# A four-layer kernel on one core: first stage on bare ternary matrices, its first chunk projected early, and unused matrix products in two preparations

## The reference

```
xn = layernorm(x)
# attention part: gates, a linear recurrence over time, a gated MLP
h   = rms_norm(xn) ;  gate = gelu(h Wg + bg) ;  hs = h Wh + bh
r, i = sigmoid(h Wr + br), sigmoid(h Wi + bi)
a   = exp(-8 softplus(alpha) r) ;  s = sqrt(1 - a*a) * hs * i
o_t = a_t * o_(t-1) + s_t                      # scan over the tokens of a sequence
hs2 = o * gate + xn ;  h2 = rms_norm(hs2)
attn = (h2 Wfc + b) * gelu(h2 Wmg + b) @ Wout + bout + hs2
# feed-forward part, on xn: weights rounded to -1, 0, 1 and scaled by row
bitlinear(x, w): scale = max(mean|w|, 1e-5) ; x @ (clip(round(w/scale), -1, 1) * scale).T
h = bitlinear(xn, w_fc) + gate0 * (xn V' B' U')          # rank 16
ffn = bitlinear(relu(h)**2, w_proj)
x = x + attn + ffn
# second layer: a selective scan (mamba) and 8 experts, top 2 of 8
```

## Time and profile before

| | us |
|---|---|
| median of 3 runs | 2524.14 (2521.16 to 2524.48) |
| the profiled execution, whole | 2515.11 |
| its span, first to last instruction | 2513.2 |
| PE busy | 2127.5 (85%) |
| DVE busy | 1925.2 (77%) |
| ACT busy | 1364.5 (54%) |
| POOL busy | 1208.3 (48%) |

### The profile page before, as it was taken

The page is one execution under the profiler, slowest core; times in us unless marked ns, Lnnn a source line. Parts: engine busy times, 40 slices in busy tenths (PEclk is TensorE's granted clock), DMA queues, the critical chain, the costliest instruction groups (busy, mean ns, idle before and its releaser), DMA issues. The chain is left out here.

```text
span 2513.2 us, 38213 instructions
## 1 busy us (share of the span) xinstructions
PE 2127.5 (85%) x12306; PEld 1716.6 (68%) x12306; DVE 1925.2 (77%) x2430; ACT 1364.5 (54%) x2421; POOL 1208.3 (48%) x889
## 2 busy tenths in 40 slices
PE   2699999999977778787878888866599999999995
PEld 1577777787752445455545555545499999999995
DVE  6554565545642899999999999999498888888883
ACT  1332233222324576767676676654377777777772
POOL 1112221122201879889797979797123333333333
PEclk8899999999988879898989798967799999999998
DMA  8010111101122322232323232323266666666663
GB/s 269 17 43 0 42 42 42 42 0 42 42 69 71 106 76 80 102 109 72 121 78 104 78 122 79 100 93 132 91 217 232 230 206 232 226 209 233 225 207 88
DMA packets 108983, 286.86 MB, mean 114 GB/s; under 512 B 20550, under 2 KB 85462, under 8 KB 90022
## 3 DMA queue, kind: packets, MB, share of 16 engines
q1 hardware_dynamic: 94598, 267.12, 30.5%
q0 software_dynamic: 14304, 18.75, 3.6%
HBM read 239.21 MB, written 50.82 MB: 115 GB/s over the span
## 5 line engine op out<-in xcount | busy, mean ns | idle before, releaser
L1102 POOL TENSOR_TENSOR m_work<-m_ux,m_bb 128x1024 f32<-128x1024 f32 x256 | 600.1, 2360 | 72.4 <-DVE m_hh L1411 63.8
L1259 ACT ACTIVATE m_da<-m_dl,m_A 128x512 f32<-128x512 f32 (+1 forms) x512 | 332.1, 681 | 198.7 <-DVE m_hh L1411 197.4
L1852 PE MATMUL e_h<-e_xTh,e_w1h 128*128 128x256 f32 x1248 | 353.2, 283 | 8.2 <-DVE e_xTl L1788 6.7
L1852 PE MATMUL e_h<-e_xTl,e_w1h 128*128 128x256 f32 x1248 | 349.2, 280 | 0.0
L1852 PE MATMUL e_h<-e_xTh,e_w1l 128*128 128x256 f32 x1248 | 349.1, 280 | 0.0
L1421 DVE TENSOR_TENSOR m_work<-m_hh,m_cb 128x1024 f32<-128x1024 f32 x256 | 312.7, 1221 | 37.3 <-PE m_cb L1502 16.0
L1531 PEld LDWEIGHTS m_y<-m_ident,m_work 128*128 128x128 f32 x2048 | 289.9, 162 | 56.8 <-issue 40.2
L1531 PE MATMUL m_y<-m_ident,m_work 128*128 128x128 f32 x2048 | 323.9, 310 | 1.2 <-DVE m_work L1421 1.2
L1411 DVE TENSOR_TENSOR_SCAN m_hh<-m_da,m_carry,m_work 128x1024 f32<-128x1024 f32 x128 | 300.0, 2344 | 6.4 <-ACT m_work L1270 6.4
L1411 DVE TENSOR_TENSOR_SCAN m_hh<-m_da,m_work 128x1024 f32<-128x1024 f32 x128 | 292.2, 2283 | 10.9 <-ACT m_carry L1280 6.3
L281 POOL TENSOR_TENSOR small<-mv,eps_ln 128x4 f32<-128x4 f32 x17 | 3.4, 200 | 550.4 <-DVE mv L399 550.4
(11 more groups left out here) (278 smaller groups left out, 4912.4 us busy)
## 6 DMA issues: line engine op xcount, KB each, us to landing
m_bb<-scratch_bT SPq DMA_DIRECT2D x64, 1024.0 KB, 4.9
m_first<-in_w SPq DMA_DIRECT2D x20, 2048.0 KB, 7.5
e_w<-in_w SPq DMA_DIRECT2D x19, 2048.0 KB, 7.6
m_first<-in_w SPq DMA_DIRECT2D x20, 1024.0 KB, 10.3
e_w<-in_w SPq DMA_DIRECT2D x19, 1024.0 KB, 10.3
scratch_rec<-x1p SPq DMA_DIRECT2D x39, 260.0 KB, 8.4
e_xg<-scratch_rec SPq DMA_DIRECT2D x39, 260.0 KB, 2.8
e_b<-in_b SPq DMA_DIRECT2D x39, 128.0 KB, 3.1
```

Of the source, the lines that this page charges most:

```text
L1102: pool.tensor_tensor(bx[:, u % NB], ux[:, cols], slot.to_broadcast([P, HALF, T]), ALU.mult).then_inc(s_bx, 1)
L1259: act.activation(da[u % NA][:, i, i:T], dl[q % 2][:, e, i:T], ACT.Exp, scale=A[:, at:at + 1]).then_inc(s_exp, 1)
L1852: last = mm(hbank[m % HR][:, j], w[i][:, k, cols], x[i][:, k], start=(p == 0 and k == 0 and j == 0), stop=(p == 2 and k == KD - 1 and j == 1),
```

## The change

1. **The ternary matrices stay bare.** `w_t` and `w_j` hold -1, 0 and 1 in fp32r. The scale of `w_f`'s rows goes into the relu (`scale=scale_col`), and the scale of `w_j` is multiplied in on DVE when O is summed. An F group is four products and one for the rank-16 part (`u_hl` with `zx`) in the place of six; `zx` comes from a new group ZX of four products in `project`.
2. **O in fp32r.** The squared relu is split into `fTh` (ACT, Square) and `fTl` (POOL), and each fp32 product with `w_j` becomes two fp32r products into the other half of the bank. Each quarter has a bank of its own.
3. **Preparation.** The loads are split over six semaphores in the order of need, chunk 0's rows are turned and projected as soon as `w_p` and the scales are there, and the halves of `w_m` and the sign product of `w_j` are made inside chunk 0. The 39 writes come behind the load of chunk 1's rows. `hn` is written over `xt`, and other tiles share memory.
4. **The last chunk** is written out apart (`more=False`): it neither centres nor projects rows of a ninth chunk.
5. **Unused products** (`warm`, and 24 in `mamba`) on TensorE.

```diff
-    order = ([f"F{m}" for m in range(FMS)] + ["MS"] + ... + ["O0", "O1"]
-             + ["XT0", "XT1", "HT0", "HT1", "R0", "R1", "I0", "I1", "H0", "H1", "GA0", "GA1"]
+    order = ([f"F{m}" for m in range(FMS)] + ["MS"] + ... + [f"O{s}" for s in range(SUB)]
+             + ["HT0", "HT1", "XT0", "XT1", "R0", "R1", "I0", "I1", "ZX", "H0", "H1", "GA0", "GA1"]
...
 # SP
-            for dst, src in w_loads:
-                sp_.dma_start(dst, src).then_inc(weights_in, 16)
+            for dst, src in small_loads:
+                sp_.dma_start(dst, src).then_inc(small_in, 16)
+            sp_.dma_start(w_f, dram["w_f"]).then_inc(wf_in, 16)
+            sp_.dma_start(w_p, dram["w_p"]).then_inc(wp_in, 16)
+            sp_.dma_start(sign_j, dram["w_j"]).then_inc(wj_in, 16)
+            sp_.dma_start(w_m, dram["w_m"]).then_inc(wm_in, 16)
...
+            wait_filled(sp_, "HT1", -1)
+            sp_.dma_start(xt[:], rows(dram["x"], 1)).then_inc(x_in, 16)
...
 # POOL, per chunk, behind row_scales
-                    wait_drained(pool, f"F{m}", c)
-                    pool.tensor_tensor(fT[:, m], fT[:, m], fT[:, m], ALU.mult).then_inc(s_fsq, 1)
+                    pool.wait_ge(s_fh, c * KH + (m + 1))
+                    pool.tensor_tensor(relu_f[m], relu_f[m], relu_f[m], ALU.mult).then_inc(s_fsq, 1)
+                    pool.wait_ge(s_fsq, c * KH + (m + 1))
+                    pool.tensor_tensor(fTl[:, m], relu_f[m], f32(fTh[:, m]), ALU.subtract).then_inc(s_fl, 1)
...
 # ACT, relu
-                    inc_drained(act.activation(fT[:, m], ps(f"F{m}")[:], ACT.Relu), f"F{m}")
+                    inc_drained(act.activation(relu_f[m], ps(f"F{m}")[:], ACT.Relu, scale=scale_col[:, 0, m:m + 1]), f"F{m}")
+                    wait_drained(act, f"F{m}", c)
+                    act.activation(fTh[:, m], relu_f[m], ACT.Square).then_inc(s_fh, 1)
...
 # DVE, sums of O (and, in chunk 0 alone, ternary_j behind h2l)
+                if first:
+                    ternary_j()
...
+                for s in range(SUB):
+                    wait_filled(dve, f"O{s}", c)
...
+                    dve.tensor_tensor(tern_out[:, s % 2], ps(f"O{s}")[:, D:2 * D], scale_j[:, 0], ALU.mult).then_inc(s_to, 1)
+                    inc_drained(dve.tensor_tensor(x1[:, s], ps(f"O{s}")[:, 0:D], xres[:, s], ALU.add), f"O{s}")
...
+                    dve.tensor_tensor(x1[:, s], x1[:, s], tern_out[:, s % 2], ALU.add).then_inc(s_x1, 1)
...
 # PE
+            def warm(n):
+                for _ in range(n):
+                    mm(bank[5][:, 0:P], ident[:], inv_d[:], start=True, stop=True)
...
+                    if name == "H":
+                        wait_bank(pe, "ZX", c)
...
-                        for m in range(KH):
-                            if s == 0:
-                                pe.wait_ge(s_fsq, c * KH + (m + 1))
-                            mm(out, fT[:, m, cols], w_j[:, m], start=False, stop=False, skip_group_check=True)
+                    for m in range(KH):
+                        if s == 0:
+                            pe.wait_ge(s_fl, c * KH + (m + 1))
+                        mm(tern, fTh[:, m, cols], w_j[:, m], start=False, stop=False, skip_group_check=True)
+                        mm(tern, fTl[:, m, cols], w_j[:, m], start=False, stop=False, skip_group_check=True)
...
-                project(c)
+                if more:
+                    project(c)
...
 # mamba, PE
+            pe.wait_ge(s_id, 2)
+            for _ in range(24):
+                mm(da[0][:, 0, 0:P], ident[:], ident[:], start=True, stop=True)
             pe.wait_ge(w_si_in, 16)
```

More of the change, by code:

```diff
@@ new lines, in _ @@
+            turned_h(-1)
+            dve.wait_ge(p_prep, PREPT["spread"])
+            for a in range(2):
+                half = slice(a * T, (a + 1) * T)
+                dve.tensor_tensor(low_u[:, half], low_u[:, half], bank[6 + a][0:LR], ALU.mult).then_inc(s_prepd, 1)
+            low_x(-1)
+            for a in range(2):
+                masked(a)
+                ternary(a)
+            dve.wait_ge(s_prepa, PREPA["u_h"])
+            dve.tensor_tensor(u_hl[4 * RANK:LR], low_u[4 * RANK:LR], f32(u_hl[4 * RANK:LR]), ALU.subtract).then_inc(s_prepd, 1)
@@ L512, in _, with low_gates @@
             dve.wait_ge(s_const, 8)
-            with dve.Fori(0, NCH) as c:
+            def low_gates():
+                for k in range(KD):
+                    dve.wait_ge(s_prepa, PREPA["w_mh"] + k)
+                    dve.scalar_tensor_tensor(out=w_ml[:, k], in0=w_m[:, k],
+                                             scalar=vec[:, V0["norm2_w"] + k:V0["norm2_w"] + k + 1], in1=f32(w_mh[:, k]),
+                                             op0=ALU.mult, op1=ALU.subtract).then_inc(s_ml, 1)
@@ L514, in _, with ternary_j, chunk @@
+            def ternary_j():
+                dve.wait_ge(s_prepd, PREPD["mask_j"])
+                dve.wait_ge(s_prepa, PREPA["sign_j"])
+                dve.tensor_tensor(w_j[:], f32(w_j[:]), sign_j, ALU.mult).then_inc(s_wj, 1)
+            def chunk(c, more, first=False):
                 for k in range(KD):
@@ L612, in _ @@
[L612 to L616 removed]
+                    last = mm(bank[1 + a][:], inv_d[:], abs_f[:, k, a], start=(k == 0), stop=(k == KD - 1))
+                last.then_inc(p_prep, 1)
+            for m in range(KH):
+                at = m % (KH // 2) * P
+                for k in range(KD):
+                    last = mm(bank[3][:, m:m + 1], abs_f[:, k, m // (KH // 2), at:at + P], inv_d[:, 0:1], start=(k == 0),
+                              stop=(k == KD - 1))
@@ L662, in _, with chunk @@
             project(-1)
-            for p in range(after, len(order)):
-                b = p % BANKS
-                pe.wait_ge(drained[b], p // BANKS)
+            for g in order[after:]:
+                b, i = place[g]
+                pe.wait_ge(drained[b], i)
                 pe.sem_inc(filled[b], 1)
                 pe.sem_inc(drained[b], 1)
-            with pe.Fori(0, NCH) as c:
-                def x_ready(part, k):
-                    if part == 0:
-                        pe.wait_ge(s_xTh, c * KD + (k + 1))
-                    else:
-                        wait_drained(pe, f"XT{k}", c - 1)
+            pe.wait_ge(s_prepa, PREPA["abs_j"])
+            for k in range(KH):
+                last = mm(bank[7][:, 0:D], inv_h[:], abs_j[:, k], start=(k == 0), stop=(k == KH - 1))
+            last.then_inc(p_prep, 1)
+            def chunk(c, more):
                 def h2_ready(part, k):
@@ L713, in _ @@
+                if more:
+                    project(c)
+                else:
+                    for g in order[first:after]:
+                        b, i = place[g]
+                        pe.wait_ge(drained[b], c * uses[b] + (uses[b] + i))
+                        pe.sem_inc(filled[b], 1)
+                        pe.sem_inc(drained[b], 1)
                 pe.wait_ge(s_l1, c * 12 + 8)
```

452 lines of the change are left out of this document (281 added, 171 removed).

## The result

Eight timed runs of each kernel: 2529.63 us (2527.62 to 2533.64) against 2523.32 us (2516.98 to 2526.77) before, a ratio of 1.0034 with an interval of 1.0024 to 1.0044. The change made the kernel slower by a third of a per cent, where 2491 was forecast. The profiled execution spans 2527.9 us against 2513.2.

A forecast was written before the change was run, and what follows sets the result against it. The prediction saw the preparation as one chain with no engine full, and PE setting most of the eight chunks. Its terms summed to -32.8 us, taking the median from 2524.14 to 2491, range 2471 to 2514.

The forecast's parts named there:

- the preparation gains less: Rival: loads land late before the first scan, 25 us gained in place of 44.7, giving 2511; chance 0.10.
- Preparation: Stretch before the first scan: scan starts near 52.5 us in place of 97.18, -44.7 (-38 to -48).
- ZX and MS: Per chunk: ZX's four added products in seven `project(c)`, +6.6; MS slower after longer PE idling, +0.75 a chunk, +5.2.
- O, chunks 0 to 6: Faster fp32r products, but the first quarter waits for POOL's `fTl` and the clock falls: +0.6 a chunk, +4.2 for seven.
- ternary_j: Chunk 0: this 2,048-wide DVE work delays the statistics, and so POOL: +2.4.
- POOL's pairs: Rival: each POOL instruction in seven chunks takes longer, at 1.5 us making the kernel slower, 2544; chance 0.04.
- the chunks gain too: Rival: PE keeps its clock through O's wait and MS stays at 1.95, 17 us better, 2474; chance 0.14.
- Chunk 7: Last chunk: POOL done before O, -6.3, but stretching DVE's chain by 5 (0 to 10.7): -1.3.
- The end of the stage: From the last O to the logits' store: 16.5 us without `project`, -3.5 (0 to -6).
- mamba: Start of the second stage: 24 unused products lift the clock for its first records, -1.7 (0 to -2).
- signs given for being wrong: POOL's subtraction taking much more than a square, PE's clock holding through the wait, or the first gates waiting for ACT.

The follow-up runs named there:

- e4: The changed kernel with four place and share tiles in the expert stage instead of two: 2512.52 us, ratio 0.9969 to the kernel before.
- e10: The changed kernel run once more, unchanged: median 2510.60 us over four runs, ratio 0.9950 to the kernel before.
- e5: The kernel of e4 with POOL's eight squares of a chunk moved to ScalarE, POOL keeping the subtractions: 2444.19 us.
- e6: The kernel of e4 with POOL's pairs in chunk 7 held back until DVE's h2l is done: 2498.90 us.

## Why the prediction was wrong, step by step

The sum was -32.8. At the experts' fast pace the change is worth 9 to 10 us (e4, e10), so some 23 us of the sum were wrong, nearly all of them in the first stage: its logits came 6.7 us earlier in the two profiles (8.2 in the mean of five profiles with either first stage), not 31. The other 17 us came from a stage that the prediction did not look at. At the fast pace the time, 2511 to 2513, lies just inside the range of 2471 to 2514, but by luck: the upper end was taken from the rival in which the preparation gains less, and the preparation gained all that was forecast.

**Preparation: right.** -44.7 forecast, -44.5 measured, with the first transposes at 22.2 (22.5 forecast).

**ZX and MS: right.** MS took 2.71 to 3.67 us in chunks 1 to 6, 3.2 in the mean, where it had been 2.3; +0.9 against the +0.75 that I took, 5.5 us in all for 5.2. The second profile of the kernel before has 2.65 in the mean, which makes it +0.55. ZX's four products start 0.23 us apart, 6.4 us for seven chunks, where 6.6 was the forecast and 6.1 are left of the 33.0.

**O, chunks 0 to 6: the mechanism right, the size wrong.** The last `w_o` products of O start 61.2 us behind the scan in chunk 0, where it was 56.7, and 57.8 to 59.6 in the others, where it was 54.9 to 56.0. Less what MS lost, that is +4.5 in chunk 0 and +2.8 in the mean of the other six, 21.4 in all; for this (O and `ternary_j`) I had 4.2 + 2.4. The 15 us between are nearly all O's: +0.6 a chunk was the forecast, +2.8 the measurement. In the chunk shown above the eighth low half comes at 41.8 in the place of 39.9. These 1.9 us are nearly all the subtraction, at 1.29 us, which I had priced like a square; the last pair at half clock adds 0.4; and `w_o` behind the wait took 4.07 to 5.28 us in the seven chunks, 1.9 us more than its 2.75 in the mean, about what I had put down for the clock (1.7). The rival "POOL's pairs" named the right term and was given 0.04: the sum was to turn at 0.29 us more for each POOL instruction. They took about 0.12 more each (a pair 2.39 us in the mean, where the sum had 2.15), less than half of that, but 13 us in 112 instructions. e5 confirms the whole of it: with eight subtractions alone the wait and the half clock are gone, and a chunk is 9.4 us shorter. The rival that "the chunks gain too", with PE keeping its clock, was plainly wrong: 0.50 was granted.

**Chunk 7: the upper bound was the truth.** I took 5 us of a range from 0 to 10.7 for POOL beside DVE's chain. The chain became 11.5 us longer: two-input instructions went from 0.65 to about 1.55 us each, the reciprocal, with one input, kept its 3.35, and the square that POOL ran beside its last 0.8 us kept its 1.04. Some 0.9 of the 11.5 is MS, which took 3.75 us, not 1.96, after PE had waited 8.8 us: DVE's wait for the reciprocal went from 2.34 to 3.21. Behind the chain the first of MG's products came 0.43 us apart in the place of 0.23. So O began 14.2 us later behind the scan, took 6.4 less (6.3 forecast), and ended 7.8 later. The Trainium skill, "SBUF — State Buffer", section "SBUF: two separate sides", says that a VectorE instruction with two SBUF inputs and a GpSimd instruction that reads SBUF share a port, which the one that starts first holds for its whole instruction while the other is blocked. The traces agree: with 0.65 and 1.04 us by themselves, the two took 1.6 and 1.5 side by side, and the one-input reciprocal was not held up. By that rule the sum would have been 5.7 us worse, which is the better forecast. The number of inputs is not all that counts, though: the centring of the earlier trace rows, with one tensor input, took 1029 ns beside POOL's squares. e6 shows the cause: with the two kept apart, the chain is 17.7.

**The end of the stage: right** (-3.0 for -3.5). **`mamba`: too much.** PE had been idle for 2.5 us between the last unused product and the first real one, and the first four records took 3.53 us against 3.75.

**The steps that failed.** Three terms of the sum: O in chunks 0 to 6 with `ternary_j`, 21.4 us for 6.6, since POOL's subtraction was priced like a square; chunk 7, +7.8 for -1.3, since DVE's chain was taken to lose 5 us and lost 11.5; and one that is not written down, that the code behind the change keeps its time, put at nothing without a reason. The experts have two paces 17 us apart, and the range did not hold them. Of the signs given for being wrong, a subtraction that takes more than a square came true, by a quarter.

## What to carry to other kernels

Price a new instruction by its own kind, operands and types, not by its neighbour on the engine, and where a wait makes TensorE work in short bursts, add the work behind the wait at half clock. Work moved onto GpSimd can cost twice: by its own length where TensorE waits for it (e5, which takes half of it away, gains 9.4 us a chunk), and by holding up VectorE's two-input chain where that runs beside it (in e6 a later start of the same work saved 12.5 us in one chunk). And when an unchanged stage differs between two profiles, look for a loop through a DMA before blaming the change; a kick of 2 us in the old kernel is a cheap test.

## What the runs showed of the hardware that was not expected

A scatter with accumulation that is in flight together with weight loads landed in 6.5 to 8.1 us in the median of some profiles and in 9.8 to 9.9 of others, by whether it was issued behind the weight load or ahead of it, and the loop of waits kept either order. Pairs of products one every 2.34 us did not keep TensorE's clock up: 0.77 was granted from 259 to 263 us and 0.50 from 263 to 267. A subtraction on GpSimd with an fp32r output took 1.26 to 1.30 us for 128x512 in chunks 1 to 6, a square in fp32 1.04; which of operand count and type makes the difference was not tried.
